# The product that spreads an expert's weights over the partitions: 128 rows with zeros in place of 16

## The reference

```python
x = x + tanh(g_xattn) * xattn(layernorm(x), ctx)       # 16 heads of 8, 1500 keys per batch
x = x + tanh(g_ffn) * ffn(layernorm(x))

# ffn, t = 448 tokens, 8 experts, 2 of them per token, F = 512
probs = softmax(t @ gate_w.T); topw, sel = top_k(probs, 2)
combine = sum(one_hot(sel) * topw / sum(topw))          # (448, 8)
gate, up = split(t @ gate_up_w[e].T)
out = sum_e combine[:, e] * ((up * gelu(gate)) @ down_w[e].T)
```

## Time and profile before

| | us |
|---|---|
| median of 3 runs | 289.96 (289.75 to 289.96) |
| the profiled execution | 289.38 |
| its span, first to last instruction | 287.6 |
| TensorE busy | 275.9 (96%) |
| VectorE busy | 214.9 (75%) |
| ScalarE busy | 181.9 (63%) |
| GpSimd busy | 97.5 (34%) |

### The profile page before, as it was taken

The page is one execution under the profiler, slowest core; times in us unless marked ns, Lnnn a source line. Parts: engine busy times, 40 slices in busy tenths (PEclk is TensorE's granted clock), DMA queues, the critical chain, the costliest instruction groups (busy, mean ns, idle before and its releaser), DMA issues.

```text
span 287.6 us, 8051 instructions
## 1 busy us (share of the span) xinstructions
PE 275.9 (96%) x2826; PEld 222.6 (77%) x2826; DVE 214.9 (75%) x420; ACT 181.9 (63%) x370; POOL 97.5 (34%) x113
## 2 busy tenths in 40 slices
PE   7988999999999999999999998999889999999994
PEld 3465878878878888887887887987688788888862
DVE  5678797797877977979679788797256988877761
ACT  2636776687677776777668666566518778775400
POOL 4598732332062043033233201032600755454200
PEclk9999999999999999999999999999999999999999
DMA  7397945943971990892695499100000000000001
GB/s 252 100 206 194 223 107 167 244 132 102 239 203 17 267 252 1 225 236 76 157 233 147 88 219 309 38 0 2 2 2 0 1 2 0 0 1 0 0 0 32
DMA packets 9924, 32.19 MB, mean 112 GB/s; under 512 B 2576, under 2 KB 3088, under 8 KB 9904
## 3 DMA queue, kind: packets, MB, share of 16 engines
q1 hardware_dynamic: 9472, 31.60, 43.1%
q10 hardware_dynamic: 432, 0.33, 0.3%
HBM read 13.26 MB, written 0.23 MB: 47 GB/s over the span
## 4 chain that ended last, share of the span: by engine, by line
PE 87%; DVE 7%; DMA 2%; ACT 1%; issue 1%; POOL 1%; SPq 0%; DVEq 0%; ACTq 0%
PE max_ps L969 16%; PE score_ps L949 14%; PE o_ps L983 14%; PE misc_ps L937 8%; PE misc_ps L931 5%; PE score_ps L1194 3%; PE score_ps L1196 3%; PE score_ps L1195 3%; DVE part_max L704 2%; PE o_ps L1194 2%; PE o_ps L1280 2%; PE o_ps L1195 2%; PE o_ps L1196 2%; PE max_ps L992 2%; PE misc_ps L1107 1%; PE max_ps L999 1%
## 5 line engine op out<-in xcount | busy, mean ns | idle before, releaser
L704 DVE TENSOR_REDUCE part_max<-max_ps 112x1 f32<-112x512 f32 (+1 forms) x192 | 117.3, 670 | 33.4 <-PE max_ps L969 31.5
L515 ACT ACTIVATE probs<-score_ps 128x448 f32<-128x448 f32 x192 | 92.0, 545 | 16.0 <-PE score_ps L949 15.9
L969 PE MATMUL max_ps<-kx,qx 96*112 96x512 f32 (+1 forms) x192 | 81.9, 432 | 2.2 <-DVE part_max L704 1.1
L949 PEld LDWEIGHTS score_ps<-qx,kx 104*128 104x128 f32 (+1 forms) x384 | 69.1, 188 | 10.7 <-issue 2.1
L949 PE MATMUL score_ps<-qx,kx 104*128 104x224 f32 (+1 forms) x384 | 73.7, 276 | 0.6 <-DVE qx L723 0.4
L983 PE MATMUL o_ps<-probs,v_sb 128*32 128x112 f32 (+1 forms) x1536 | 44.5, 261 | 0.6 <-ACT probs L515 0.6
L969 PEld LDWEIGHTS max_ps<-kx,qx 96*112 96x112 f32 x192 | 33.6, 176 | 8.7 <-issue 4.9
L983 PEld LDWEIGHTS o_ps<-probs,v_sb 128*32 128x32 f32 (+1 forms) x1536 | 36.4, 110 | 3.1 <-ACT probs L515 0.8
L366 POOL TENSOR_TENSOR k_low<-k_full,k_high 128x512 fp32r<-128x512 f32 (+1 forms) x21 | 26.2, 1252 | 30.7 <-ACT k_full L498 30.4
L399 POOL TENSOR_TENSOR o_norm<-o_sb,inv_den 128x112 f32 (+1 forms) x15 | 6.3, 423 | 75.8 <-DVE inv_den L730 75.8
L510 ACT ACTIVATE v_sb<-misc_ps 128x512 f32<-128x512 f32 x24 | 14.4, 601 | 27.4 <-PE misc_ps L937 27.4
(11 more groups left out here) (177 smaller groups left out, 369.0 us busy)
## 6 DMA issues: line engine op xcount, KB each, us to landing
kx<-k_high SPq DMA_DIRECT2D x60, 187.5 KB, 5.2
kx<-k_low SPq DMA_DIRECT2D x30, 187.5 KB, 5.1
ctx_sb<-in_ctxT SPq DMA_DIRECT2D x7, 750.0 KB, 5.7
gu_sb<-in_guT SPq DMA_DIRECT2D x8, 512.0 KB, 5.5
dn_sb<-in_dnT SPq DMA_DIRECT2D x8, 256.0 KB, 5.3
ctx_sb<-in_ctxT SPq DMA_DIRECT2D x2, 256.0 KB, 4.3
kx<-k_high SPq DMA_DIRECT2D x4, 123.5 KB, 2.3
kx<-k_high SPq DMA_DIRECT2D x4, 64.0 KB, 2.0
```

The costliest lines, as they stand in the source:

```text
L515: nc.scalar.activation(probs[:, (KT * h + t) % 8, :], score_ps[:, t % 3, 0:SC // 2], ACT.Exp, scale=SCALE).then_inc(exp_done, 1)
L704: nc.vector.reduce_max(part_max[:, p, c:c + 1], max_ps[0:PC, bank, 0:size], AX.X).then_inc(max_taken, turns)
L949: last = nc.tensor.matmul(score_ps[0:m, t % 3, GC * g:GC * g + GC], kx[0:KR, 2 * par + h, g, 128 * t:128 * t + m], qx[0:KR, par, 2 * h + g ...
L969: nc.tensor.matmul(max_ps[0:PC, bank, 0:size], qx[0:MR, par, 2 * h + p // 2, PC * (p % 2):PC * (p % 2) + PC], kx[0:MR, slot, p // 2, start ...
```

## The change

The selector and `combT` get 128 rows. `combT` becomes a tensor of its own; GpSimd clears all of it once, at the end of its preparations, and ScalarE later fills the first 16 rows as before. The row mask gets 128 rows x 8 (the two diagonals of ones still lie in the first 16 rows). The table `expert_sel` and VectorE's copy that made it are gone: GpSimd widens one column of the mask to 128 columns for each expert, in 128 rows. The spread product takes 128 rows on both sides; rows 16 to 127 are zero. GpSimd's wait for the table becomes a wait for the mask.

```diff
+ROWS = 128
@@ tensors
-        row_mask = sb("row_mask", [16, NP])
+        row_mask = sb("row_mask", [ROWS, NP])
-        expert_sel = sb("expert_sel", [16, E, 128], f32r)
-        expert_now = sb("expert_now", [16, 2, 128], f32r)
+        expert_now = sb("expert_now", [ROWS, 2, 128], f32r)
-        combT = q_parts[0:16, 0, :]
+        combT = sb("combT", [ROWS, TOK], f32r)
@@ GpSimd
             ones_rows(3)
 
+            serial(nc.gpsimd.memset(combT[:, :].bitcast(f32), 0.0))
+
             def select(e, par):
-                nc.gpsimd.tensor_copy(expert_now[:, par, :], expert_sel[:, e, :].bitcast(f32)).then_inc(select_ready, 1)
+                nc.gpsimd.tensor_copy(expert_now[:, par, :], bc(row_mask[:, e].unsqueeze(1), [ROWS, 128])).then_inc(select_ready, 1)
-            pool.wait_ge(select_all, 1)
+            pool.wait_ge(rows_ready, 1)
@@ ScalarE
-            nc.scalar.activation(combT, max_ps[0:16, 1, 0:TOK], ACT.Copy).then_inc(combT_saved, 1)
+            nc.scalar.activation(combT[0:2 * E, :], max_ps[0:2 * E, 1, 0:TOK], ACT.Copy).then_inc(combT_saved, 1)
@@ VectorE, called in the first layer norm
-            def copy_selectors():
+            def add_masks():
                 dve.wait_ge(heads_ready, 1)
                 nc.vector.tensor_reduce(head_mask[:, :], head_mask3[:, :, :].rearrange("p g h -> p h g"), AX.X,
                                         ALU.add).then_inc(mask_ready, 1)
-                dve.wait_ge(rows_ready, 1)
-                nc.vector.tensor_copy(expert_sel[:, :, :], bc(row_mask[:, :].unsqueeze(2), [16, E, 128])).then_inc(select_all, 1)
@@ TensorE, spread_weight
-                nc.tensor.matmul(max_ps[:, par, 0:TOK], expert_now[:, par, :], combT, start=True, stop=True
+                nc.tensor.matmul(max_ps[:, par, 0:TOK], expert_now[:, par, :], combT[:, :], start=True, stop=True
```

More of the change, by code:

```diff
@@ L176, in flamingo_block @@
         kx_loaded = [[sem(f"kx_loaded{u}{g}") for g in range(2)] for u in range(4)]
-        consts, mask_ready, select_all, cleared, pool_step = map(sem, ("consts", "mask_ready", "select_all", "cleared", "pool_step"))
+        consts, mask_ready, cleared, pool_step = map(sem, ("consts", "mask_ready", "cleared", "pool_step"))
         scratch_ready = sem("scratch_ready")
@@ L746, in copy_selectors @@
                                         ALU.add).then_inc(mask_ready, 1)
-                dve.wait_ge(rows_ready, 1)
-                nc.vector.tensor_copy(expert_sel[:, :, :], bc(row_mask[:, :].unsqueeze(2), [16, E, 128])).then_inc(select_all, 1)
-            layer_norm(x_sb, 1, 0, NR, copy_selectors)
+            layer_norm(x_sb, 1, 0, NR, add_masks)
             def q_rest(g):
```

## The result

| | before, same chip | after |
|---|---|---|
| median of 5 runs, us | 289.75 (289.44 to 289.96) | 287.95 (287.29 to 288.83) |
| ratio, 95% interval | | 0.9942 (0.9920 to 0.9963) |
| run again later, 6 runs | 289.76 | 287.38 (286.98 to 288.01), ratio 0.9892 (0.9851 to 0.9934) |
| profiled execution (span) | 289.38 (287.6) | 288.83 (287.1) |

The change makes the kernel faster by 1.8 us, or 2.4 us in the second series. The forecast was 2.5 us, to 287.45 us. The ratios are the record's own; the two medians of the second series alone give 0.9918.

What follows compares the result with a forecast made beforehand. TensorE was taken as the bound, busy almost all the time with 87% of the last-ending chain. Expert stage 2.06 plus start 0.45 made 2.51 us, from 289.96 to 287.45 us; range 286.8 to 288.6.

Steps and rivals of the forecast that it cites:

- The gap belongs to the shape: Spread product of 16 rows among 128-row neighbours loses 0.41 us on TensorE; 128 rows should remove it.
- The argument from the product of 112 rows and that of 16 columns: Same stage: distance stays 0.21 us into 112 rows, 0.30 into 16 columns, so only small array corners cause gaps.
- The ring of 7.56 us: Experts 1 to 3: loop PE to VectorE to GpSimd limits an expert to 7.56 us; gain 1.04 us in all.
- PE's 7.50 us in experts 4 and 5: VectorE has less work there, so TensorE's 37 products at 0.203 us bound the expert; gain 0.41 us each.
- Expert 0 at nothing: TensorE's down product behind the spread waits for the same VectorE subtraction regardless, so gain 0.
- Expert 6: VectorE, idle until the spread is done, starts earlier by 0.09 plus 0.11 us; gain 0.20 us.
- The selector at nothing: GpSimd's selector copy, widened to 128 rows, stays at 0.28 us; value 0, bounds -0.2 to +1.2 us in all.
- The price of 0.1 us of ring for 0.1 of selector: Experts 0 to 3: each 0.1 us more of selector copy adds up to 0.1 us to the ring.
- The start, 0.45 us: Without VectorE's table copy beside it, GpSimd's power shortens from 1.48 to 1.035 us, passing 0.45 us to the end.
- Three columns and one gave four by a straight line: GpSimd's power at the start: 0.875 us for three columns, 0.555 for one, so 1.035 for four.
- The estimate by the Trainium skill: At the start, the page's 115 ns after the copy's end puts the power's end at 7.08 us, gain 0.69.
- The expert stage: Gains of experts 0 to 6 together: 0 + 1.04 + 0.82 + 0.20 = 2.06 us, bounds 1.5 to 2.3.

Runs made afterwards that it cites:

- the early selector: Changed kernel with GpSimd copying the next expert's selector before its wait for the scaled tokens: 287.53 us, ratio 0.9925; with two filler rounds as well, 287.40 us.

## Why the prediction was right, and where its terms were off

The direction, the mechanism and the range held: 287.95 and 287.38 us for 287.45.

- **The gap belongs to the shape: shown**, by 64 and 96 rows. At all seven places the starts are now 0.20 to 0.21 us apart, in and out; in expert 0 the way out had been covered by a wait for DVE. The argument from the product of 112 rows and that of 16 columns was enough to forecast it.
- **The ring of 7.56 us: right as a ring, and not what bound this profile.** With 96 rows experts 1 to 3 took 7.56 to 7.57 with DVE's waits at 1.03 to 1.04. In the kernel after they took 7.56 to 7.62, forecast 1.04 us of gain and measured 0.92; PE had no idle time before `up`, and the missing 0.12 us is PE's pace, the term below. That expert 2 took exactly 7.56 is a coincidence of two bounds that lie 0.02 us apart.
- **PE's 7.50 us in experts 4 and 5: the mis-sized term.** They took 7.63, so 0.56 us came for 0.82. The step that failed is (7.91 - 0.41) / 37 = 0.203 us taken as PE's pace whatever stands around it. Without the gap PE runs at 0.203 in some stretches and at 0.207 in others, at the same granted clock. Which one a stretch has differs between kernels (with the early selector experts 4 and 5 had 7.51 and 7.50, then 7.57 and 7.63 in a second kernel with it) and between executions of one (expert 2 of the kernel after: 7.56, then 7.63). What decides it stays open. That a pause in the stream keeps the quick pace would fit: the gap gave one, and with the selector made twice, where PE started `up` 0.26 to 0.38 us late in experts 2 to 4, experts 4 and 5 took 7.59 and 7.50. But in the kernel after the pace also goes from 0.207 to 0.202 us at 240.32 without a pause that the trace shows, and no run tests it.
- **Expert 0 at nothing: too low by 0.14 us.** The spread's own part was right: with 96 rows there is no gap and expert 0 takes 8.93 us for 8.92. The step took POOL's and DVE's order there as fixed, and it tips in every kernel with 128 rows in the selector.
- **Expert 6: 0.27 for 0.20 us**, with DVE's wait for the spread 0.81 us, where the earlier trace rows had 0.98.
- **The selector at nothing: right for its own time**, 0.291 us for 0.282, apart from expert 0. The price of 0.1 us of ring for 0.1 of selector was somewhat high: 0.2 for 0.29.
- **The start, 0.45 us: right in the trace, not resolved in the time.** Three columns and one gave four by a straight line: 1.035 us for 1.030. "Its other inputs are in by then, so I let the 0.45 us through to the end" is the weak step: it holds where PE is ready and no transfer further on is late. PE's opening filler ends at 5.65 in one execution and at 7.02 in another, and in one an earlier PE waited for context at 53 us. The copy put back cost nothing measurable with three fillers, and about 0.5 with two. That the copy lengthens the power was argued from the earlier trace rows and is now shown, with the size that the rows had; that it does so by holding a port stays an explanation that no run here tests. The estimate by the Trainium skill, page "SBUF — State Buffer", section "A bandwidth-pool intuition that's wrong (but worth ruling out)", was 0.69 us, and the measured 0.45 decides against it.

**The sum.** The expert stage gave 1.89 us for 2.06. The medians fell by 1.80 and 2.38, which leaves -0.1 to 0.5 us for the start: its 0.45 is inside and can't be read closer. That the medians lie so near the forecast is in part luck: the pace took 0.38 us off the stage, expert 0 and expert 6 gave 0.21 more than forecast, and the start is not resolved.

## What to carry to other kernels

A lone product of 16 or 64 rows in a stream of full ones cost TensorE twice here, going in and coming out, 0.41 us in all; padding its operands with zeros to 96 or 128 rows cost no time on the engine (same columns) and removed both. Before counting the gain, read the next-longest ring from the trace, since the rings and PE's own pace kept 0.06 to 0.13 us of each steady expert's 0.41 us here. And an edit that frees an engine at the start of a kernel is worth its trace time only if the engine it feeds is ready: look at what that one does in several executions, and at the next transfer it will wait for.

## What the runs showed of the hardware that was not expected

- A product of 64 rows has the whole gap of one of 16 rows, and one of 96 rows has none.
- Two paces of one gapless stream of 448-column products, 0.203 and 0.207 us, at a granted clock of 1.00 throughout.
- PE's first microseconds at half pace (0.85 us between products that later stand 0.43 apart) with the granted clock recorded at 1.00, ending anywhere from 4.5 to 7.9 us after the start in the profiles with three rounds of fillers, and at about 13.6 with one.
- A drop to 0.50 (1.2 GHz) for about 3 us in two of fourteen profiled executions, at the same place, behind an idle time of 1.15 to 1.17 us that the twelve others had as well without a drop. In the kernel after it cost 1.5 us, most of what the change gained.
- POOL's pair of subtractions in expert 0 took 2.55 to 2.57 us behind a selector of 16 to 96 rows and 2.95 to 2.97 behind one of 128 rows, with DVE's first subtraction done between the two only there.
